# A four-stage kernel: the third stage on the second's 16-position tiles, filled inside the second's last steps, with pair products on four quadrants of partitions

## The reference, cut to what matters

```python
# stage c, per sequence
x_ssm, z = split(layernorm(x) @ W_in)
x_ssm = silu(causal_conv(x_ssm, conv_w, K=4) + conv_b)
dt = softplus(x_ssm @ dt_w + dt_b);  B = x_ssm @ B_w;  C = x_ssm @ C_w
def step(h, t):                        # h: 128 channels x 16 states
    h = h * exp(dt[t] * A) + (dt[t] * x_ssm[t]) x B[t]
    return h, sum_s(h * C[t])
y = (scan(step) + x_ssm * D) * silu(z);  return x + y @ W_out
```

## Time and profile before

| | |
|---|---|
| median of 3 runs | 1071.47 us (1069.3 to 1071.88) |
| profiled execution | 1073.75 us, span 1071.9 us |
| PE busy | 887.4 us (83%) |
| DVE busy | 671.8 us (63%) |
| ACT busy | 572.0 us (53%) |
| POOL busy | 492.8 us (46%) |
| granted PE clock, mean | 0.839 of full speed |

### The profile page before, as it was taken

The page is one execution under the profiler, slowest core; times in us unless marked ns, Lnnn a source line. Parts: engine busy times, 40 slices in busy tenths (PEclk is TensorE's granted clock), DMA queues, the critical chain, the costliest instruction groups (busy, mean ns, idle before and its releaser), DMA issues.

```text
span 1071.9 us, 21820 instructions
## 1 busy us (share of the span) xinstructions
PE 887.4 (83%) x8032; PEld 712.3 (66%) x8032; DVE 671.8 (63%) x2014; ACT 572.0 (53%) x1033; POOL 492.8 (46%) x893
## 2 busy tenths in 40 slices
PE   1777778276999999998657888998849999999995
PEld 0766667165888888877535565655537888878785
DVE  3566665366588888875329998989856155180622
ACT  1434343133667666665366897977826354362631
POOL 1366665322255455434368899999840002020111
PEclk9856565555789999999867998888959999999998
DMA  9100000110000000000020000000000000000000
GB/s 307 39 10 15 10 15 17 40 50 1 2 6 12 7 12 6 12 12 11 10 84 1 1 1 1 1 1 0 2 0 1 1 1 20 1 20 0 1 20 20
DMA packets 30707, 20.67 MB, mean 19 GB/s; under 512 B 2960, under 2 KB 28952, under 8 KB 30368
## 3 DMA queue, kind: packets, MB, share of 16 engines
q1 hardware_dynamic: 25984, 12.59, 4.1%
q10 hardware_dynamic: 4640, 6.99, 1.9%
...
## 4 chain that ended last, share of the span: by engine, by line
PE 57%; POOL 19%; DVE 10%; issue 6%; ACT 5%; DMA 1%; ACTq 1%; POOLq 0%; SPq 0%; DVEq 0%
PE ps L1108 12%; PE ps L1109 9%; PE ps L1110 9%; PE ps L1121 6%; PE ps L1183 6%; POOL prod L529 5%; POOL term L514 4%; PE ps L1442 3%; PE ps L1176 2%; PE ps L1127 2%; PE ps L1103 2%; POOL c_ln_rs L119 2%; DVE wall L985 2%; POOL a_ln_rs L113 1%; PE ps L1160 1%
## 5 line engine op out<-in xcount | busy, mean ns | idle before, releaser
L112 POOL TENSOR_TENSOR d_ln_ve<-d_ln_mv,eps 128x4 f32<-128x4 f32 x16 | 3.2, 202 | 238.7 <-DVE d_ln_mv L106 238.7
L1108 PE MATMUL ps<-h_h,wh_h 128*128 128x512 f32 x256 | 99.6, 389 | 0.0
L1109 PE MATMUL ps<-h_h,wh_l 128*128 128x512 f32 x256 | 99.6, 389 | 0.0
L1110 PE MATMUL ps<-h_l,wh_h 128*128 128x512 f32 x256 | 99.6, 389 | 0.0
L1183 PE MATMUL ps<-w_e,he 128*128 128x128 f32 x512 | 83.3, 300 | 5.1 <-ACT he L618 4.8
L1121 PEld LDWEIGHTS ps<-mov,hbd 32*128 32x128 f32 x2048 | 85.4, 251 | 0.0
L1121 PE MATMUL ps<-mov,hbd 32*128 32x32 f32 (+1 forms) x2048 | 83.1, 324 | 0.0
L618 ACT ACTIVATE he<-ps,pp 128x256 f32<-128x256 f32 x128 | 59.8, 472 | 43.1 <-PE ps L1110 38.1
L1183 PEld LDWEIGHTS ps<-w_e,he 128*128 128x128 f32 x512 | 73.1, 211 | 7.7 <-ACT he L618 7.0
L529 POOL TENSOR_TENSOR prod<-bcT 16x256 f32<-16x256 f32 (+7 forms) x128 | 69.0, 567 | 6.3 <-ACT bcT L738 6.3
L1086 DVE TENSOR_TENSOR d_y<-ps,w_s 128x512 f32<-128x512 f32 x8 | 5.5, 691 | 102.5 <-PE ps L1442 102.5
...
## 6 DMA issues: line engine op xcount, KB each, us to landing
...
```

The costliest lines, as they stand in the source:

```text
L1108: pe.matmul(dst, a_h, b_h, start=start, stop=True, skip_group_check=True)
L1109: pe.matmul(dst, a_l, b_h, start=False, stop=True, skip_group_check=True)
L1110: return pe.matmul(dst, a_h, b_l, start=False, stop=True, skip_group_check=True)
```

## The change

Stage c works on the tiles of b: a tile is 16 positions of all 16 sequences, two chunks per sequence, and it stays in `xB`. The store to `x2`, the wait for it and the load by sequence are gone. Since the positions of a sequence now lie in 16 tiles after each other, state and convolution tail are handed on from tile to tile: the scan over chunks becomes four products and sums on DVE (`carried`, `states`), and ACT copies the last three positions of the tile before (`transposed_input`). The output is stored by position, four transfers of 64 KB where there was one of 256 KB.

```diff
-                    dve.tensor_tensor_scan(hc[l][:, 1:1 + DS * NCH], flat3(d0[l][:, :, :]), ps[:, STATE, :], 0.0,
-                                           ALU.mult, ALU.add).then_inc(S["c_hs"], 1)
+            def carried(t):
+                if t == 0:
+                    dve.wait_ge(zero_ready, 3)
+                else:
+                    dve.wait_ge(S["c_hs"], t)
+                chain.link(dve.tensor_tensor(hd[:, :, :], hc[t % 2][:, :, 0:NB], decay(t, 0), ALU.mult))
+            def states(t):
+                l = t % 2
+                dve.wait_ge(S["c_st_ps"], t + 1)
+                state = ps[:, STATE, :].rearrange("p (n c) -> p n c", c=NCH)
+                chain.link(dve.tensor_tensor(hc[l][:, :, NB:NCH], hd[:, :, :], state[:, :, 0:NB], ALU.add))
+                chain.link(dve.tensor_tensor(hd[:, :, :], hc[l][:, :, NB:NCH], decay(t, 1), ALU.mult))
+                dve.tensor_tensor(hc[1 - l][:, :, 0:NB], hd[:, :, :], state[:, :, NB:NCH], ALU.add).then_inc(S["c_hs"], 1)
```

```diff
-                    for j in range(CH):
-                        last = pool.tensor_tensor(
-                            prod[l][:, OFF[j]:OFF[j + 1]].rearrange("p (c t) -> p c t", t=CH - j),
-                            bcT[l][:, 1, :, j:CH], bcT[l][:, 0, :, 0:CH - j], ALU.mult)
+                pool.tensor_tensor(wide, c_t.unsqueeze(1).to_broadcast([P, HALF, 8, CH]), shifted(l, HALF, CH), ALU.mult)
+                pool.tensor_tensor(thin, c_t[:, :, HALF:CH].unsqueeze(1).to_broadcast([P, HALF, 8, HALF]),
+                                   shifted(l, 0, HALF), ALU.mult).then_inc(S["c_prod"], 1)
-                    for b, (j0, j1) in enumerate(PAIR_BANKS):
-                        last = pe.matmul(ps[:, PAIRS + b, 0:OFF[j1] - OFF[j0]], ones[0:DS, :], prod[o][:, OFF[j0]:OFF[j1]],
-                                         start=True, stop=True)
+                for g in range(4):
+                    last = pe.matmul(ps[:, PAIRS + g, 0:BC_AT], ones[heads(g), :], prod[l][heads(g), :],
+                                     start=True, stop=True)
```

```diff
+            def fill(n, place):
+                if place == 0 and n == NB - 3:
+                    transposed_input(0)
+                if place == 1 and n == NB - 3:
+                    silus(0)
+                    normed(0)
+                if place == 0 and n == NB - 2:
+                    parts_of_step(0)
+                    in_and_out(0)
+                    transposed_input(1)
+                if place == 1 and n == NB - 2:
+                    chain.clear()
+                    log_part(0)
+                    silus(1)
+                    normed(1)
+                if place == 1 and n == NB - 1:
+                    decays(0)
```

```diff
+                if n == NB + 2:
+                    low_parts(2)
+                    low_parts(3)
...
+            for n in range(0, NB + 3):
+                step_c(n, within(n))
+                if n == NB - 1:
+                    step_d(-1, 0, within(-1, ITER_MLP))
```

844 lines of the change are left out of this document (521 added, 323 removed).

## The result

| | us | ratio to the kernel before, 95% interval |
|---|---|---|
| kernel before (20 runs) | 1071.63 median (1067.29 to 1077.19) | 1 |
| changed kernel (20 runs) | 1068.92 median (1066.16 to 1070.93) | 0.9971 (0.9959 to 0.9983) |
| forecast | 1045 (1023 to 1061) | 0.975 |

The account below looks back on a forecast made before the run. POOL was taken to bound the middle of c, DVE right behind it. 1073.75 - 20.7 (A) - 6.5 (B) + 0 (C) + 0.3 (output) = 1046.8, less 2.3 for the median, put as 1045 us; range 1023 to 1061.

Parts of the forecast that it names:

- Part A: Seam from b to c: first `term` 38.0 us earlier, against 17.3 us added in b's last steps; net -20.7 us.
- sum of fills: Work newly placed in b's last steps on ACT, PE, DVE and POOL: together 17.3 us, from 14 to 21.
- Statistics on DVE, scales and fills with zeros on POOL: In b's steps 11 to 14: taken as 1.0 us, both engines being busy 10 of 28 us there.
- Part B: Stage c's fifteen intervals from first to last `term`, 202.0 us before: -6.5 us, from +8 to -20.
- The relief of POOL: Stage c: `prod` falls from 4.9 to about 1.1 us per step, POOL stops being the bound, DVE regains 0.65.
- ten full intervals: Those of c's fifteen intervals taken to gain 0.75 to 0.8 us each; POOL never bounded the other five.
- Part C: Seam from c to d: d's first product 5 us early, the gain taken as eaten; 0, from -4 to +4.
- Output: Very end: four transfers of 64 KB for one of 256 KB; +0.3 us, from 0 to +1.
- Rival 1: Stage c: DVE is set free, its hidden waits nearly all go, a step of 12.4 us; 1031 us, chance 0.22.
- Rival 2: Only the seam pays: DVE's step stays 14.3 us, c unchanged or 2 us more; 1055 us, chance 0.20.
- rival 3: PE's clock falls in c and PE overtakes DVE, up to 1096 us; chance 0.05 slower, 0.02 meeting the old time.
- Rival 4: Table loads and fills through b cost what they save: A -8, B nothing; 1063 us, chance 0.05.

Follow-up runs that it names:

- e2: Changed kernel with POOL's scales of stage c behind b's third power function and the zeros of `wall` one step later: 1063.14 us, ratio 0.9925.
- e3: Changed kernel with Gelu replacing Silu for tiles 0 and 1, and Exp and Ln for tile 0, so six table loads fall away: 1057.99 us, ratio 0.9872.
- e10: Changed kernel with ACT's fills in b's last steps in another order, some Silu and the normed pair of tile 1 moved: 1063.00 us, ratio 0.9924.
- e12: Changed kernel with the edits of e1, e2, e4, e5, e10 and the first `hd` product on POOL, computation complete: 1042.18 us, ratio 0.9717.
- e15: Kernel before, with POOL making only the last of eight products per tile after the first two tiles: 1057.17 us, ratio 0.9860.
- e14: Changed kernel with one scan over 512 state columns in place of the four state operations of a tile: 1055.10 us, ratio 0.9846.
- e5: Changed kernel with the chunk-end decays written by ACT into their own tile, which the two `hd` products read side by side: 1062.44 us, ratio 0.9924.
- e6: Changed kernel without POOL's seven sums over the source positions: 1055.34 us, ratio 0.9860.
- e11: Changed kernel with POOL making each tile's products three times into the same place: 1081.23 us, ratio 1.0077.
- e7: Changed kernel with d's first preparation moved back behind c's last step on all four engines: 1075.67 us, ratio 1.0038.
- e4: Changed kernel with POOL's two subtractions of 2048 columns (large low parts) each made as four of 512: 1065.14 us, ratio 0.9934.
- e1: Changed kernel with the last round's eight output transfers issued by two queues, SP's and ACT's: 1066.20 us, ratio 0.9943.

## Why the prediction was wrong

**Part A** was put at -20.7 us (-24 to -17); with the 1.4 us that this execution was ahead at tile 11 it is -14.0 by the time of the first `term`, 562.03 against 575.99. Its large term held, from the prediction: "the first `term` would come 10.1 us after b's last sum", measured 10.9. What failed is the sum of fills, 17.3 us with ends at 14 and 21, measured 24.6. Two of its terms are at fault. "Statistics on DVE, scales and fills with zeros on POOL ... I take 1.0" was argued from POOL's idle time; e2 shows 6.6 us (5.8 by medians), not by POOL's load but by its order: the scales stand ahead of the power functions for which DVE, POOL, PE and ACT wait in turn. I had looked at the zeros (1.8 us each, 0.4 us of cost) and not at who is queued behind the scales. And the 7.7 us of table loads were taken less 3.1 us of idle time that they were to fill, where e3 gives 11.3: the loads whole, and with them the stretches at the low clock. What stays for everything else is 24.6 - 6.6 - 11.3 = 6.7 us, if the two add, as e2 and e10 did in e12. The 24.6 is itself not sharp: against the 55.5 us of e15's execution the fills cost 20.6, the upper end of what was forecast.

**Part B** was put at -6.5 us (+8 to -20) and is +4.4. Right: `prod` at 1.3 us, PE's pair products as a block of 0.93 us, DVE above 93%, `wall` at 3.0 us and no idle behind PE that decides. POOL fell only to 75%, not to the 60 to 65 forecast: its sums, taken as unchanged, grew by 1.1 us per step. In e15 they grew too (a mean of 538 ns for 458), though only the products were gone, so a part of it is what they run beside; no run takes it apart. DVE's step is 14.0 us instead of 13.5 to 13.6. The term that failed is the scan of 1.21 us that "becomes four of about 0.42: +0.5". The rows say +1.07, and e14 prices it at 14.8 us for the 15 intervals, where I had 7.5. The size 0.42 came from products with one operand in PSUM; two of the four read two SBUF tiles, the decays among them with a pitch (e5: 0.2 us in each product), and one of the two stands beside POOL's sums (e6: 0.16). The relief of POOL, end of its bound and 0.65 us of waits, was implied at about 14 us; e15 gives 14.6 us for 4.6 us of `prod`, and e11 11.0 us for 2.5 us put back, so it was sized about right. Scaled to the 3.6 us of `prod` that the change took away (4.9 to 1.3), e15 makes it 11.4 us, an estimate. So -14 + 7.5 = -6.5 became -11.4 + 14.8 = +3.4; the other 1.0 us I cannot assign by a run. `c_ya` (0.59 against 0.48) and `c_xq` (0.47 against 0.42, twice) are longer now, and `c_yi` shorter by 0.32. Of `c_xq` e6 shows the cause: without POOL's sums it takes 0.33.

A check was missed, too. 15 steps of 13.5 us are 202.5 us, which is the 202.0 of before: the 14.3 us held in the middle alone, in seven intervals and not in the "ten full intervals" of the prediction (e15 gains in the same seven). Before, the full intervals from 651.58 to 753.47 are 14.6 us, the first six 12.6 and the last two 12.3; now these are 14.0, 13.5 and 13.6. The change did gain in the middle (3.7 us over seven) and lost at both sides (5.4 and 2.7), where DVE's longer work meets no bound of POOL that it could replace.

**Part C** was put at 0 (-4 to +4) and is +2.5. The mechanism is the one named: the first product 17.4 us behind the last `term` (forecast 17), then DVE's low parts of 2.40 and 4.41 us beside POOL's two. e7 shows the early preparation worth 6.5 us, e4 that POOL's long instructions cost at least 3.2 us. Only the size is a little off, and inside the range.

**Output**, put at +0.3 (0 to +1), is +4.1. I counted four transfers in place of one for one lane; there are two lanes, eight issues on one queue at 0.85 us each, and the second lane's four stand behind the first's. e1 returns 3.1 of it.

**Rivals.** Rival 1 did not come: DVE is not set free, though e6 shows that the time is there. Rival 2 comes nearest to what decided B (c costs 2 us more, since new instructions bring their own waits), but what they brought was the pitch and POOL's sums (e5, e6), and it has A and the end too cheap. Of rival 3 a piece is seen: the clock in the middle of c went from 0.88 to 0.77, PE idling 14.1 us in 100 for DVE's `hc` (row below), but PE did not overtake DVE, and the clock cost where the rival did not look, in b's end. Rival 4 has A at -8; with 1063 us it was nearest to the measured 1069, apart from the 0.02 given to rival 3 for just meeting the old time. The misses, 7.3 and 0.9 in A, 10.9, 2.5 and 3.8 us, less the 1.4 of the start, are the 24 us between 1045 and 1069. All of them are on one side: new work was priced at the shortest row of its size, or at nothing where an engine idled. Two small slips of adding change nothing: 1046.8 less 2.3 is 1044.5 and not 1044.7, and the range of 1036 to 1054 comes out only if the three spreads are added as squares; added straight they give some 1031 to 1060, which still leaves 1069 out.

```profile
L1632 PE MATMUL ps<-ident,hc 128*128 128x128 f32 x28 | 5.8, 334 | 14.1 <-DVE hc L1189 14.1
```
